# Delta's short convolution and its filters on TensorE, with part of the quantising and the first context groups sent ahead

## The chip, the cores and the metric

The kernel runs on one core of one Trainium2 chip, all of it in fp32 and in one launch. The metric is the time of one execution on the device, in microseconds (us); lower is better. A core has TensorE (PE), VectorE (DVE), ScalarE (ACT), GpSimd (POOL) and the sync engine (SP), each with its own stream of instructions, and 16 DMA engines that all queues share. The changed kernel runs under the same conditions.

## The reference, cut to what matters

The program is a Perceiver with four layers of three blocks each on `x` [128, 256] and a context `ctx` of 12544 rows of 256. Each block is `x = x + block(layernorm(x))`. The blocks that the change touches:

```
# layer 0: slot attention over ctx (3 iterations), parameter attention, then a quantised FFN
w  = clip(round(wb / s), -8, 7) * s     # blocks of 32 weights, s = max|wb| / 7, for w_up, w_gate, w_down
# layer 1: softmax attention over ctx with padding, then folded attention and experts
# layer 2: 16-head attention over ctx with a mask, then the delta block:
q = silu(dwconv(h @ Wq, conv_w_q))      # causal, depthwise, 4 taps; k and v likewise
beta = sigmoid(h @ Wb)
inv = solve_triangular(I + tril(kb @ k.T, -1), I)          # q, k normalised per head, kb = k * beta
delta_out = tril(q @ k.T) @ (inv @ (v * beta))             # 4 heads of 64; what crosses chunks is elided
local_short = dwconv(v, fir_short_w)    # 5 taps
local_long  = dwconv(v, fir_long_w)     # 64 taps
o = gated sum of local_short, local_long, delta_out, v;  o = rmsnorm(o) @ Wo
# layer 3: softmax attention over ctx (plain), multi-query attention, hashed experts
```

## The kernel before, in words

Twelve stages run one after the other: slots, patt (parameter attention), quant (the quantised FFN), padded, folded, moe, cross, delta, local, plain, mqa, hashed. A stage is one `nc.Block` in which each engine has its own program, written by hand in the order in which it runs; semaphores order the engines within a stage, and a barrier stands between stages. All stages but slots start with the layer norm of `x_kept` on DVE and ACT. Weights live in one region of SBUF (`K.weights`, `HOMES`; `weights_region` in rows) and are fetched by a DMA issued a stage or more ahead, mostly from SP's queue.

The context is read in 14 groups of 896 rows (`GROUPS`, `GROUP`). In padded and plain, `CtxAttention.sync` sends the transposed group `ctxT`, double buffered, from the start of its own stage; `CtxAttention.tensor` scores a group (`product`, L142), turns the probabilities (L1016) and attends (L1027). The cross stage projects keys and values of each group on PE into a ring of banks (L142, `cross_ring`), scores with 16 heads in sets (L1761) and DVE takes masked maxima in halves (L1921). There the SP queue holds `w_delta`, then `ctxT` and the mask of each group in turn, and POOL turns each mask into fp32 (L1725).

In patt, DVE quantises all weights of the FFN between its other work: `quantise_some(n)` takes the next n of 42 steps, 7 kinds (L757 to L769) on 6 pieces of 768 columns, and `Q_SPLIT` says how many go at each of nine places. In quant, PE transposes the quantised weights in lots of three (L913), ACT copies them out (L895), and the activations are quantised by a maximum over all partitions, which POOL makes (L904).

In delta, PE makes q, k and v with channels in the rows. DVE does the 4-tap convolution as 24 instructions (`tap`, L2188 for a first tap, L2189 for the others), ACT the sigmoid (L2146), PE transposes the product into token rows (L2074, L2076), and DVE normalises q and k (to L2230). The filters of 5 and 64 taps are 138 more instructions of `tap`, put by `filter_some` between the steps of the inverse. The inverse of `I + A` is built in 6 levels, each with the chain: DVE `E` (L2250), PE `E I` (L2098), DVE copy (L2253), PE `I E I` (L2108, L2109), DVE two subtractions (L2262, L2263). After it come `u` (L2113, L2266) and `delta_out` (L2117), then the statistics and gates of the four branches. `idle_products` (L158) are products whose result nobody reads.

## Time and profile before

| | |
|---|---|
| median of 3 runs | 1695.83 us (1695.51 to 1701.81) |
| profiled execution, its own time | 1700.65 us |
| its span | 1698.9 us |
| PE, DVE, ACT busy in the span | 1443.1, 966.7, 713.4 us |
| mean granted TensorE clock | 0.915 |

The profile is one execution, 4.8 us (0.3%) above the median; 1.8 us of its own time lie outside its span. Busy shares are means over twelve stages with different limits, so each stage is read by itself. The stages start, by their layer norms, at about 338 (patt), 405 (quant), 448 (padded), 562 (folded), 618 (moe), 689 (cross), 1304 (delta), 1434 (local), 1542 (plain), 1650 (mqa) and 1677 us (hashed).

### The profile page before, as it was taken

The numbers are of one execution on the slowest core, as the hardware profiler recorded it, in microseconds if no ns is written. First come the engines' busy times: TensorE is split into PE (matmuls) and PEld (weight loads), VectorE is DVE, ScalarE is ACT, GpSimd is POOL, SyncE is SP. The second block draws the span as 40 slices with busy tenths as digits, with TensorE's granted clock in tenths as the row PEclk, the third lists the DMA queues.
The fourth block names the chain that finished last, engine by engine and source line by source line (L and its number), as shares of the span: only waits on it lengthen the run. The fifth ranks groups of instructions, "written<-read, shape, count | busy, mean of one in ns | idle before, by whom it ended". The sixth has DMA issues, their size and how long they took to land. (4 is left out here: it accounts for less than half of the span.)

```text
span 1698.9 us, 28391 instructions
## 1 busy us (share of the span) xinstructions
PE 1443.1 (85%) x10880; PEld 1076.8 (63%) x10880; DVE 966.7 (57%) x2914; ACT 713.4 (42%) x1618; POOL 91.9 (5%) x86
## 2 busy tenths in 40 slices
PE   7999989886499867799999999999995455677997
PEld 6878979763267643467777777777764352545765
DVE  4654444465566312367777777777774873453433
ACT  5745535422122100166666666666663101212222
POOL 2300000000000200200000000000000000000000
PEclk9999999977699879899999999999998565998998
DMA  9935424110332469410010100000002002506830
GB/s 324 328 143 193 152 68 150 49 51 20 120 135 87 173 250 392 180 42 34 34 34 34 34 34 34 34 34 34 2 1 121 1 0 87 227 0 240 274 108 4
DMA packets 63318, 181.16 MB, mean 107 GB/s; under 512 B 7248, under 2 KB 43216, under 8 KB 61904
## 3 DMA queue, kind: packets, MB, share of 16 engines
q1 hardware_dynamic: 59488, 160.96, 26.4%
q0 software_dynamic: 3264, 12.58, 1.9%
q10 hardware_dynamic: 432, 5.80, 0.8%
q8 instruction: 88, 1.44, 0.3%
q14 instruction: 46, 0.38, 0.1%
HBM read 178.68 MB, written 0.66 MB: 106 GB/s over the span
## 5 line engine op out<-in xcount | busy, mean ns | idle before, releaser
L1849 ACT ACTIVATE cross_s<-cross_s,cross_shift 128x896 f32<-128x896 f32 x224 | 215.1, 1031 | 35.1 <-DVE cross_shift L1930 35.1
L1843 ACT COPY cross_eT<-cross_ring 128x512 f32<-128x512 f32 x280 | 153.1, 591 | 145.1 <-PE cross_ring L1769 145.1
L1769 PEld LDWEIGHTS cross_ring<-consts,cross_s 128*128 128x128 f32 x1568 | 170.8, 142 | 59.1 <-issue 43.8
L1769 PE MATMUL cross_ring<-consts,cross_s 128*128 128x128 f32 x1568 | 199.4, 280 | 8.7 <-ACT cross_s L1849 8.7
L1921 DVE CUSTOM_DVE_ANT_0 cross_s<-cross_scores,cross_mask,cross_top 128x448 f32<-128x448 f32 x224 | 141.3, 681 | 84.3 <-PE cross_scores L1761 84.3
L387 ACT ACTIVATE slots_probs<-slots_scores,slots_bias,ctx_rinv 128x128 f32<-128x128 f32 x294 | 130.1, 461 | 111.4 <-DVE slots_bias L432 111.4
L1921 DVE CUSTOM_DVE_ANT_0 cross_s<-cross_scores,cross_mask,cross_half_max 128x448 f32<-128x448 f32 x224 | 141.2, 680 | 18.9 <-PE cross_scores L1761 18.9
L142 PE MATMUL slots_scores<-slots_qkT,slots_ctxT 128*128 128x128 f32 x1176 | 140.9, 279 | 10.1 <-DMA slots_ctxT<-in_ctxT 9.3
L142 PEld LDWEIGHTS slots_scores<-slots_qkT,slots_ctxT 128*128 128x128 f32 x1176 | 139.4, 195 | 14.0 <-DMA slots_ctxT<-in_ctxT 10.2
L337 PE MATMUL slots_attended<-ctx_rows,slots_probs 128*128 128x257 f32 x588 | 135.1, 380 | 1.4 <-DVE slots_pooled L446 1.4
L1761 PE MATMUL cross_scores<-cross_keysT,cross_qz 32*128 32x448 f32 x896 | 119.1, 589 | 0.8 <-DVE cross_keysT L1895 0.8
L337 PEld LDWEIGHTS slots_attended<-ctx_rows,slots_probs 128*128 128x128 f32 x588 | 108.2, 190 | 17.7 <-DVE slots_probs L442 3.6
L428 DVE TENSOR_REDUCE slots_top<-slots_scores 128x7 f32<-128x896 f32 x42 | 45.9, 1092 | 116.8 <-PE slots_scores L142 116.7
L1783 PEld LDWEIGHTS cross_attended<-cross_eT,cross_values 128*32 128x32 f32 x3136 | 82.3, 110 | 37.9 <-issue 35.8
L1783 PE MATMUL cross_attended<-cross_eT,cross_values 128*32 128x128 f32 x3136 | 97.2, 274 | 2.3 <-ACT cross_eT L1843 1.7
L142 PE MATMUL cross_ring<-cross_ctxT,weights_region 128*128 128x448 f32 x224 | 92.0, 555 | 6.8 <-DMA cross_ctxT<-in_ctxT 6.8
L1903 DVE COPY cross_eT<-cross_ring 128x512 f32<-128x512 f32 x112 | 77.4, 691 | 35.5 <-PE cross_ring L1769 35.5
L142 PE MATMUL cross_ring<-weights_region,cross_ctxT 128*128 128x256 f32 x392 | 90.9, 384 | 0.0
L142 PEld LDWEIGHTS cross_ring<-weights_region,cross_ctxT 128*128 128x128 f32 x392 | 72.3, 190 | 10.4 <-issue 0.7
L1725 POOL TENSOR_SCALAR cross_mask<-cross_mask_int 128x896 f32<-128x896 int32 x14 | 44.9, 3207 | 471.0 <-DVE cross_top L1921 460.9
L142 PEld LDWEIGHTS cross_ring<-cross_ctxT,weights_region 128*128 128x128 f32 x224 | 41.3, 194 | 41.2 <-issue 32.9
L387 ACT ACTIVATION_READ_ACCUMULATOR slots_probs<-slots_scores,slots_bias,ctx_rinv 128x1 f32 x294 | 61.1, 208 | 0.0
(762 smaller groups left out, 2073.2 us busy)
## 6 DMA issues: line engine op xcount, KB each, us to landing
slots_ctxT<-in_ctxT SPq DMA_DIRECT2D x42, 896.0 KB, 4.6
ctx_rows<-in_ctx_rows SPq DMA_DIRECT2D x28, 896.0 KB, 7.1
padded_ctxT<-in_ctxT SPq DMA_DIRECT2D x14, 896.0 KB, 4.6
cross_ctxT<-in_ctxT SPq DMA_DIRECT2D x14, 896.0 KB, 4.6
plain_ctxT<-in_ctxT SPq DMA_DIRECT2D x14, 896.0 KB, 4.6
ring_w<-in_moe_w POOLq DMA_DIRECT2D x12, 1024.0 KB, 16.2
ring_w<-in_moe_w SPq DMA_DIRECT2D x12, 1024.0 KB, 10.9
local_layers<-in_w_local SPq DMA_DIRECT2D x2, 4806.0 KB, 14.1
```

The costliest lines, as they stand in the source:

```text
L142: last = pe.matmul(out, lhs, rhs, start=i == 0, stop=i == len(pairs) - 1)
L337: last = pe.matmul(at[b], probs[:, n % HELD, t], K.ctx[:, g * TILE + t, :], start=t == 0, stop=t == TILE - 1)
L387: last = act.activation(probs[:, a, t], sc[b][:, t], ACT.Exp, bias=bias[:, a, t:t + 1], scale=K.rinv[:, g * TILE + t:g * TILE + t + 1], ac ...
L428: dve.tensor_reduce(top[:, a], sc[b], X_AXIS, ALU.max).then_inc(st("top"), 1)
L1725: pool.tensor_scalar(mask[:, g % 2], mask_int[:, g % 2], 0.0, MASKED, ALU.is_equal, ALU.mult).then_inc(st("mask"), 1)
L1761: pe.matmul(scores(j), qz[rows, s // 2, s % 2], keysT[rows, g % 2, s // 2, half_keys(half)], start=True, stop=True).then_inc(st("scored"), 1)
L1769: last = pe.transpose(bank(("turn", u, t))[:, j * P:(j + 1) * P], s_buf[:, u % 2, j, t * P:(t + 1) * P], K.ident)
L1783: last = pe.matmul(attended[COLS * j:COLS * (j + 1), s * P:(s + 1) * P], values[:, g % 2, t, set_head(s, j)], eT[:, u % 2, t, j * P:(j + 1 ...
L1843: act.copy(eT[:, u % 2, t], bank(item)).then_inc(st("emptied_act"), 1)
L1849: act.activation(rows, rows, ACT.Exp, bias=shift[:, u % 2, j:j + 1], scale=SCALE).then_inc(st("exp"), 1)
L1903: dve.tensor_copy(eT[:, u % 2, t], bank(item)).then_inc(st("emptied_dve"), 1)
L1921: dve.tensor_tensor_reduce(s_buf[:, u % 2, j, half_keys(half)], scores(j), mask[:, g % 2, half_keys(half)], 1.0, so_far, ALU.add, ALU.max, ...
```

## The change

The change has four parts.

**Delta.** The 24 taps of the convolution and the 138 of the filters become 162 PE matmuls of 128x128 with a diagonal matrix that holds the tap's weights. ACT makes the diagonals (L2229 of the kernel after, `identity * scale`) into a ring of 40 places in the weights region; each tap waits for its diagonal, and diagonal n of 40 or more waits until tap n - 40 is done. q and k leave the convolution with tokens in the rows, so their four transposes, the copy and the product `qkvT` go. DVE only copies the two filtered branches from a bank at the end, after all 162 taps.

**Quantising.** `w_up` gets its own home and fetch, issued on ACT's queue behind `w_patt` at the start of the second slots iteration; DVE quantises it in the slots stage, one or two steps of 128x384 per group, 28 in all. In patt 28 steps of 768 columns are left, in the places 2, 4, 4, 2, 2, 3, 4, 5, 2, and the transposes of `up` move from quant into patt, in place of idle products.

**Early groups.** Two groups of `ctxT` for padded, one for cross, two for plain are fetched into the weights region in the stage before (quant, moe and local). padded and plain have 4 idle products at their start. In cross, the keys of group 0 are projected from there, four pieces of them (`BANKS` = 3 ahead of the layer norm's transposes, then one), DVE stores them before it makes `qz`, and `ctxT` of group 0 leaves SP's queue.

**The fetch of `w_hashed`** moves from the local stage to the end of plain's SP queue.

```diff
+def filter_taps():
+
+    return [(kind, c, k) for kind, rows, length in (("conv", 3 * DC, CONV), ("long", DC, LONG), ("short", DC, SHORT))
+            for c in range(rows) for k in range(length)]
+
+
+DIAGONALS = 40
 
 
...
+                fir_places = iter(enumerate(taps_in_turn))
+                for n, (_, ac, k) in itertools.islice(fir_places, 3 * DC * CONV):
+                    a, c = ac // DC, ac % DC
+                    pe.wait_ge(st("raw"), a + 1)
+                    pe.wait_ge(st("diagonal"), n + 1)
+                    shifted, diagonal = raw[:, a, c, k:k + P], diagonals[:, n % DIAGONALS]
+                    if a < 2:
+                        last = pe.matmul(b[4][:, ac * P:(ac + 1) * P], shifted, diagonal, start=k == 0, stop=k == CONV - 1)
+                    else:
+                        last = pe.matmul(b[5][:, c * P:(c + 1) * P], diagonal, shifted, start=k == 0, stop=k == CONV - 1)
+                    last.then_inc(st("filtered"), 1)
                 pe.wait_ge(st("silu"), 1)
...
+                def filter_some(count):
+
+                    for n, (kind, c, k) in itertools.islice(fir_places, count):
+                        pe.wait_ge(st("diagonal"), n + 1)
+                        length, at = (SHORT, c * P) if kind == "short" else (LONG, D + c * P)
+                        lo = PAD - length + 1 + k
+                        pe.matmul(b[7][:, at:at + P], vT[:, c, lo:lo + P], diagonals[:, n % DIAGONALS],
+                                  start=k == 0, stop=k == length - 1).then_inc(st("filtered"), 1)
+
+                filter_some(22)
                 pe.wait_ge(st("unit"), 1)
                 for c in range(DC):
                     for a, src in ((0, qk[:, 0]), (1, qk[:, 1])):
...
-                    if n == LEVELS - 1:
-                        pe.wait_ge(st("firs"), 1)
-                        for a in range(2):
-                            for c in range(DC):
-                                last = pe.transpose(b[1][:, (a * DC + c) * P:(a * DC + c + 1) * P], firs[:, a, c], K.ident)
-                        last.then_inc(st("firs_mm"), 1)
+                    filter_some(4)
                     pe.wait_ge(st("EI"), n)
...
+                    filter_some(8)
...
+                filter_some(len(taps_in_turn))
                 pe.wait_ge(st("u"), 1)
...
+                def diagonal_some(count):
+
+                    for n, (kind, c, k) in itertools.islice(diagonal_places, count):
+                        if n >= DIAGONALS:
+                            act.wait_ge(st("filtered"), n - DIAGONALS + 1)
+                        act.activation(diagonals[:, n % DIAGONALS], K.ident, ACT.Copy, scale=taps_of[kind][:, c, k:k + 1]).then_inc(st("diagonal"), 1)
+
+                diagonal_some(DIAGONALS)
+                act.wait_ge(st("filtered"), 2 * DC * CONV)
+                act.activation(act_sig[:, 0:2].rearrange("p a d -> p (a d)"), b[4][:, :], ACT.Sigmoid).then_inc(st("sigmoid"), 1)
+                act.wait_ge(st("filtered"), 3 * DC * CONV)
+                act.activation(act_sig[:, 2], b[5][:, 0:D], ACT.Sigmoid).then_inc(st("sigmoid"), 1)
                 act.wait_ge(st("beta_mm"), 1)
...
+                act.wait_ge(st("sumsq"), 1)
+                act.activation(norms[:, 1, :], norms[:, 0, :], ACT.Sqrt).then_inc(st("lengths"), 1)
+                diagonal_some(len(taps_in_turn))
...
-                    filter_some(8)
                     dve.wait_ge(st("EI_mm"), n)
                     dve.tensor_copy(EI[:, :], two(b[4][:, :])).then_inc(st("EI"), 1)
-                    filter_some(14)
...
+                dve.wait_ge(st("filtered"), len(taps_in_turn))
+                link(dve.tensor_copy(z[:, 0:2].rearrange("p a h d -> p (a h d)"), b[7][:, :]))
...
-Q_SPLIT = (4, 8, 4, 2, 2, 4, 4, 4, 10)
+Q_SPLIT = (2, 4, 4, 2, 2, 3, 4, 5, 2)
...
+                        if it == 1 and 3 <= g < GROUPS:
+                            up.some(dve, 1)
+                        if it == 2 and g < GROUPS:
+                            up.some(dve, 2 if g < 4 else 1)
...
-                idle_products(pe, K, spare, 2)
+                turn_up(0)
+                turn_up(1)
...
-                idle_products(pe, K, spare, 4)
+                turn_up(2)
+                turn_up(3)
+                idle_products(pe, K, p_idle, 2)
...
+                K.weights.wait(pe, "cross")
+                for p in range(BANKS):
+                    project(("keys", 0, p))
                 pe.wait_ge(st("ln_done"), 1)
...
-                K.weights.fetch(sp, "hashed")
+                K.weights.fetch_early(sp, "plain")
...
+EARLY = {"padded": 2, "cross": 1, "plain": 2}
```

On PE, in one level of the inverse of the kernel before (`delta_bank` is the bank that a matmul writes; the pair L2108, L2109 comes once for each head, four times in all), the rows are:

```order
L2098 MATMUL delta_bank<-delta_inv,delta_E 128x128 x4
L2108 MATMUL delta_bank<-delta_EI,delta_inv 128x128
L2109 MATMUL delta_bank<-delta_inv,delta_EI 128x128
...
L2098 MATMUL delta_bank<-delta_inv,delta_E 128x128 x4
```

On the same engine the kernel after has, from the end of qkv to the first level, these rows; `weights_region` here is the ring of diagonals, `delta_raw` and `delta_vT` what is filtered:

```order
L155 MATMUL delta_bank<-weights_region,delta_hT 128x4 x2
L2137 MATMUL delta_bank<-weights_region,delta_raw 128x128 x16
L2139 MATMUL delta_bank<-delta_raw,weights_region 128x128 x8
L2143 MATMUL delta_bank<-consts,delta_vT 128x128 x2
L2152 MATMUL delta_bank<-weights_region,delta_vT 128x128 x22
L2159 MATMUL delta_bank<-consts,delta_qk 128x128 x2
...
L2152 MATMUL delta_bank<-weights_region,delta_vT 128x128 x6
...
L2152 MATMUL delta_bank<-weights_region,delta_vT 128x128 x24
L2178 MATMUL delta_bank<-delta_inv,delta_E 128x128 x4
L2152 MATMUL delta_bank<-weights_region,delta_vT 128x128 x4
L2183 MATMUL delta_bank<-delta_EI,delta_inv 128x128
L2184 MATMUL delta_bank<-delta_inv,delta_EI 128x128
...
L2152 MATMUL delta_bank<-weights_region,delta_vT 128x128 x8
L2178 MATMUL delta_bank<-delta_inv,delta_E 128x128 x4
```

So taps of L2152 stand now ahead of products that the chain waits for: 22 before the transposes of q and k (L2159), 6 and 24 about the products of A (L2170), then 4 and 8 in every level.

On ACT, from the start of delta, the kernel before has:

```order
L180 ACTIVATE delta_ln_mv<-delta_ln_mv 128x1
L2146 ACT_TABLE_LOAD
L2146 ACTIVATE delta_act_sig<-delta_act_in 128x768
L2148 ACTIVATE delta_beta<-delta_bank 128x4
L2149 ACTIVATE delta_res<-weights_region 128x4
L2151 ACTIVATE delta_temp<-weights_region 128x1
L2152 ACT_TABLE_LOAD
L2152 ACTIVATE delta_temp<-delta_temp 128x1
L2153 ACT_TABLE_LOAD
L2153 ACTIVATE delta_temp<-delta_temp 128x1
L2155 ACT_TABLE_LOAD
L2155 ACTIVATE delta_norms<-delta_norms 128x8
```

and the kernel after has there:

```order
L193 ACTIVATE delta_ln_mv<-delta_ln_mv 128x1
L2229 ACTIVATE weights_region<-consts,weights_region 128x128 x40
L2233 ACT_TABLE_LOAD
L2233 ACTIVATE delta_act_sig<-delta_bank 128x512
L2235 ACTIVATE delta_act_sig<-delta_bank 128x256
L2237 ACTIVATE delta_beta<-delta_bank 128x4
L2238 ACTIVATE delta_res<-weights_region 128x4
L2241 ACT_TABLE_LOAD
L2241 ACTIVATE delta_norms<-delta_norms 128x8
L2229 ACTIVATE weights_region<-consts,weights_region 128x128 x122
L2243 ACTIVATE delta_temp<-weights_region 128x1
L2244 ACT_TABLE_LOAD
L2244 ACTIVATE delta_temp<-delta_temp 128x1
L2245 ACT_TABLE_LOAD
L2245 ACTIVATE delta_temp<-delta_temp 128x1
```

So 40 diagonals stand ahead of the first table load and the sigmoids, and 122 behind the lengths of q and k.

## Rows read from the trace of the kernel before

**Rows 1.** Windows: length, busy of PE, PEld, DVE, ACT, POOL, clock, DMA, GB/s

```profile
689.00:1304.00 615.00, 589.70 (x6348) 419.07 (x6348) 430.80 (x1625) 401.46 (x580) 48.40 (x18) 0.98 0.10 37
1304.00:1434.00 130.00, 65.67 (x268) 51.72 (x268) 90.41 (x265) 12.89 (x21) 0.26 (x2) 0.57 0.10 40
```

**Rows 2.** Timeline of delta, head: start, us, engine, line, [idle before <-releaser]

```profile
1311.20 1.34 DVE L2183 COPY delta_raw<-delta_bank 128x256 f32<-128x256 f32 x3 [4.53 <-PE delta_bank L142]
...
1313.76 4.81 DVE L2189 SCALAR_TENSOR_TENSOR delta_act_in<-delta_raw,weights_region,delta_act_in 128x128 f32<-128x128 f32 x18
...
1319.94 0.84 ACT L2146 ACTIVATE delta_act_sig<-delta_act_in 128x768 f32<-128x768 f32 x1
...
1328.33 0.42 DVE L2230 TENSOR_TENSOR delta_kb<-delta_qk,delta_beta 128x256 f32<-128x256 f32 x1
```

**Rows 3.** Timeline of delta, the levels and what follows them

```profile
1341.18 0.69 DVE L2250 TENSOR_TENSOR delta_E<-delta_A,weights_region 128x512 f32<-128x512 f32 x1
...
1350.80 2.08 PE L2098 MATMUL delta_bank<-delta_inv,delta_E 128*128 128x128 f32 x8 [2.23 <-DVE delta_E L2250]
...
1353.65 0.80 PE L2108 MATMUL delta_bank<-delta_EI,delta_inv 128*128 128x128 f32 x2 [0.78 <-DVE delta_EI L2253]
...
1359.67 1.16 PE L2098 MATMUL delta_bank<-delta_inv,delta_E 128*128 128x128 f32 x8 [2.23 <-DVE delta_E L2250]
...
1393.79 1.10 PE L2113 MATMUL delta_bank<-delta_vb,delta_inv 128*128 128x64 f32 x8 [1.57 <-DVE delta_inv L2263]
...
1395.48 1.97 PE L2117 MATMUL delta_bank<-delta_u,delta_attnT 128*128 128x64 f32 x8 [0.59 <-DVE delta_u L2266]
```

**Rows 4.** Timeline of patt: ACT on 128x128 tiles with a scalar from memory

```profile
357.49 4.23 ACT L526 ACTIVATE patt_pr<-patt_scores,patt_small 128x128 f32<-128x128 f32 x16 [5.58 <-DVE patt_small L536]
```

**Rows 5.** Windows of two stretches, columns as in rows 1

```profile
1342.00:1350.00 8.00, 5.78 (x24) 5.19 (x24) 7.69 (x25) 0.00 (x0) 0.00 (x0) 0.50 0.00 0
...
490.00:510.00 20.00, 20.00 (x86) 14.25 (x85) 13.73 (x30) 5.12 (x12) 0.00 (x0) 1.00 0.41 138
```

**Rows 6.** Timeline of cross, start

```profile
701.07 8.54 PE L142 MATMUL cross_ring<-cross_ctxT,weights_region 128*128 128x448 f32 x16 [6.84 <-DMA cross_ctxT<-in_ctxT]
702.91 6.53 POOL L1725 TENSOR_SCALAR cross_mask<-cross_mask_int 128x896 f32<-128x896 int32 x2 [10.03 <-DMA cross_mask_int<-in_mask]
...
718.68 0.68 DVE L1921 CUSTOM_DVE_ANT_0 cross_s<-cross_scores,cross_mask,cross_half_max 128x448 f32<-128x448 f32 x1 [4.69 <-PE cross_scores L1761]
```

**Rows 7.** DMA view: transfers, count, KB each, us from issue to landing

```profile
weights_region<-in_w_hashed SPq DMA_DIRECT2D x1, 5764.0 KB, 33.1
...
weights_region<-in_w_delta SPq DMA_DIRECT2D x1, 2596.5 KB, 10.0
```

**Rows 8.** Timeline of patt: quantising steps and a product

```profile
359.94 3.52 DVE L757 TENSOR_REDUCE block_max<-weights_region 128x24 f32<-128x768 f32 x4
...
397.62 1.90 PE L738 MATMUL patt_scores<-weights_region,patt_efT 128*128 128x256 f32 x8
398.70 5.29 DVE L769 TENSOR_TENSOR weights_region<-weights_region,block_max 128x768 f32<-128x768 f32 x6
```

**Rows 9.** Timeline of padded, start

```profile
453.15 4.90 PE L142 MATMUL padded_scores<-padded_ctxT,padded_hT 128*128 128x512 f32 x8 [2.58 <-DMA padded_ctxT<-in_ctxT]
...
468.87 0.98 PE L1016 MATMUL padded_turned<-consts,padded_e 128*128 128x128 f32 x7 [1.24 <-ACT padded_e L1047]
```

**Rows 10.** Timeline of plain, start

```profile
1546.23 9.40 PE L142 MATMUL plain_scores<-plain_ctxT,plain_hT 128*128 128x512 f32 x16 [2.18 <-DMA plain_ctxT<-in_ctxT]
```

**Rows 11.** Timeline of slots and quant

```profile
136.86 3.39 PE L142 MATMUL slots_scores<-slots_qkT,slots_ctxT 128*128 128x128 f32 x28 [1.68 <-DMA slots_ctxT<-in_ctxT]
...
165.03 1.09 DVE L428 TENSOR_REDUCE slots_top<-slots_scores 128x7 f32<-128x896 f32 x1 [3.10 <-PE slots_scores L142]
...
412.89 0.38 POOL L904 PARTITION_ALL_REDUCE quant_small<-quant_small  x1 [315.48 <-issue]
```

**Rows 12.** The page's costliest groups: the line's weight loads

```profile
L1769 PEld LDWEIGHTS cross_ring<-consts,cross_s 128*128 128x128 f32 x1568 | 170.8, 142 | 59.1 <-issue 43.8
```

More of the change, by code:

```diff
@@ L645, in stage_pattention @@
         spare = mm[:, 1024:1536]
+        up_n = K.weights.buf("quant_up").rearrange("p (o i) -> p o i", i=D)
+        upT = K.weights.beyond("quant", DC * QFFN).rearrange("p (c o) -> p c o", c=DC)
+        p_idle = mm[:, 1536:2048]
+        lots = [(c, o, (spare, sc[:, 1024:1536])[n % 2]) for n, (c, o) in enumerate((c, o) for c in range(DC) for o in (0, 3))]
         with nc.Block() as block:
@@ L688, in mask, with turn_up @@
                     pe.matmul(heads[:, 4 * g:4 * g + 4], K.ident, repeat(K.causal, 4), start=True, stop=False)
+                def turn_up(n):
+                    c, o, bank = lots[n]
+                    if n >= 2:
+                        pe.wait_ge(st("up_copied"), n - 1)
+                    for j in range(3):
+                        last = pe.transpose(bank[:, j * P:(j + 1) * P], up_n[:, o + j, c * P:(c + 1) * P], K.ident)
+                    last.then_inc(st("up_mm"), 1)
                 turn("k", "k_probs")
@@ L1006, in score @@
             for lo, hi in ((0, KEYS_A), (KEYS_A, GROUP)):
-                last = product(pe, self.sc[b][:, lo:hi], [(self.qT[:, c], ctxT[:, b, c, lo:hi]) for c in range(DC)])
+                last = product(pe, self.sc[b][:, lo:hi], [(self.qT[:, c], ctxT[:, c, lo:hi]) for c in range(DC)])
             last.then_inc(st("scored"), 1)
@@ L1794, in spread_decay @@
                     last.then_inc(st("filled"), 1)
-                for p in range(KEY_PIECES):
-                    project(("keys", 0, p))
                 pe.wait_ge(st("qz"), 1)
@@ L1943, in add @@
                     dve.wait_ge(st("added"), g + 1)
-                for p in range(KEY_PIECES):
-                    store(("keys", 0, p))
                 for u in range(STEPS + 2):
@@ L2781 @@
 }
+EARLY = {"padded": 2, "cross": 1, "plain": 2}
+EARLY_AT = {"padded": HOMES["padded"][1] + width(PADDED_SPEC), "cross": HOMES["cross"][1] + width(CROSS_SPEC) + SLOT_W1 + SLOT_W2,
+            "plain": HOMES["hashed"][1]}
 REGION = max(at + width(spec) for spec, at in HOMES.values())
```

292 lines of the change are left out of this document (145 added, 147 removed).

## The prediction

> **What bounds the kernel now.** I read the page first, then the windows by stage, then the timeline of each stage that the change touches, and last the DMA view. The stages stand one behind the other, so each has its own bound and the gains add. In cross PE is busy 589.70 of 615 us: only its start can give. In delta PE is busy 65.67 of 130 us at a granted clock of 0.57, and DVE 90.41 [rows 1]. The timeline of delta shows two reasons. At its head PE waits for DVE's 24 taps, which end at 1318.6 [rows 2]. In the levels it is a chain: E, product, copy, product, two subtractions. DVE's filter taps fill only the waits of that chain, so removing them alone gains almost nothing; but PE runs its two products at the low level of its clock: eight records in 2.08 us, against 1.16 us in a level that had the high one [rows 3]. So what counts in delta is the clock, and the chain at its head. Padded and plain lose time at their start to groups of the context that are still on their way.
>
> **Delta, the head.** A product is two records: (1.16 - 0.3 for the end of the last one) / 4 gives 0.21 us a tap at the high level (2.4 GHz), (2.08 - 0.37) / 4 gives 0.43 at the low one (1.2 GHz) [rows 3]. A diagonal costs ACT 4.23 / 16 = 0.264 us, by 16 instructions of the same size that also take a scalar from memory [rows 4]. From about 1305.1, behind the layer norm, 40 of them end at 1315.7. The first copies of `raw` are done at 1311.6 [rows 2], so the 16 taps of q and k are through at 1315.0 and the 24 at 1316.7: ACT is later than PE. The sigmoid stood 1.3 us behind the last tap, a table load, so it starts at 1317.0 and, for 512 of 768 columns at 0.84 us [rows 2], ends at 1317.6, against 1320.8. From there to the end of `kb` it was 8.0 us (to 1328.75) [rows 2]; without the transposes of q and k, the wait for them and their copy it is 5.9: 1323.5, a gain of 5.2. But 22 taps stand ahead of the transposes that wait for it. They start at about 1321.2 and take 4.7 us, to 1325.9, and give back 2.4. Then the transposes and the products of A run at the high level, which gives about 1.7; the 6 taps lie beside DVE's copies, the 24 (5.1 us) beside DVE's ten instructions for A (5.7 us). The first E starts at 1336.7 instead of 1341.18 [rows 3]: **-4.5**.
>
> **Delta, the levels.** Six levels took from 1341.18 to 1393.79, 52.6 us, 8.8 each [rows 3]. At the high level the products give back 0.92 and twice that: 8.9 - 2.7 = 6.2 us. The 4 taps, 0.85 us, stand where PE waited 0.78 for DVE's copy, the 8, 1.7 us, where it waited 2.23 [rows 3]: I put 6.3 a level, 37.8 in all: **-14.8**. Is the clock high? PE would be busy over 90% of such a level. The stretches show 1.00 where PE is busy without a gap, and 0.50 where it is busy 5.78 of 8 us [rows 5]; at low clock the taps would leave PE no gap at all, which is the first case. I take the high level. Behind `u`'s product stand the last 162 - 148 = 14 taps, 3.0 us, ahead of `delta_out`'s product, which waited 0.6 for `u`, and itself becomes shorter by about 1 [rows 3]: +1.3. For 162 waits on a diagonal I add 1. **Delta: -17**. Its bounds: -21 if the waits cost nothing and all of A runs at the high level; -8 if two levels fall to the low one, at 11.0 us each (below).
>
> The Trainium skill ("ScalarE: Activation LUTs", What ACT_TABLE_LOAD costs) has about 280 ns plus 0.833 ns a column for an ACTIVATE with one pointer operand, less 93 ns back to back, or 0.294 us a diagonal where the row shows 0.264: by it 40 diagonals end 1.2 us later, and the sum would be 1 less.
>
> **Cross.** Projecting the keys of group 0 began at 701.07, when its group landed, at low clock (8.54 us) [rows 6]; it can now begin at about 688.5, right behind moe and before the layer norm. The mask comes next: in SP's queue it stands directly behind `w_delta`, issued at 688.9, which takes 10.0 us [rows 7]; the mask then took 702.91 - 701.07 = 1.8, so it lands at 700.7, POOL turns it in half of 6.53 [rows 6], and DVE's first maxima start at 704.0, four of 0.68 us later the second half at 706.6. That half started at 718.68 [rows 6], after PE had done the values; these now lie before the mask. From there the chain is the same and PE stays full to the end of the stage: -12.1, and **-11.5** for DVE's stores that now stand in its way. Bounds: -9.5 (mask and early group meet on the DMA engines, 2 us), -12.7 (all of 701.07 - 688.4).
>
> **Patt.** A quantising step of 768 columns costs DVE 3.52 / 4 = 0.88 us [rows 8]. Two steps fewer stand before the copies of the probabilities: -1.75; one fewer before the sum with `xin`: -0.9. At the end, f's product was done at 399.5 and DVE with six steps at 404.0 [rows 8]; two steps are left, and five instead of four before the last copy delay the product by 0.6: -3.9. The moved transposes take PE 6 records where four of twice the width stood: nothing. **-6.5**, from -4.5 (a stretch more at low clock) to -8.
>
> **Padded and plain.** In padded the turn of group 1 waited to 468.87, 1.24 us of it for ACT [rows 9]. Scores waited 2.58 for their first group [rows 9] and again for the second. With both there, they start some 2.0 us earlier and run on, and DVE's and ACT's chain on group 1 begins some 5.8 earlier, which sets that turn: **-5.5** (-3.7 if the products run low, -6.3). In plain the scores waited 2.18, and the sixteen records took 9.40, half of it at low clock [rows 10]; 1.6 of the wait go, and the idle products keep the clock up for about 3: **-4.5** (-2.5 to -5.5).
>
> **The rest.** In slots the 28 steps on half the columns, 0.45 us each, lie in 3.10 us that DVE waits in each group [rows 11]; but 768 KB more are fetched, and PE already waited 1.68 for a group behind `w_patt` [rows 11]: +0.5 (0 to +1.5). In quant POOL's first all-reduce starts at 412.89, about when the lots ended [rows 11]; it sets the products, so fewer lots gain nothing, and less work for PE may cost clock: +0.5 (0 to +1.5). `w_hashed`, 33.1 us with company [rows 7], is sent at about 1620 and needed at 1677 less the gains: nothing, with over 10 us of cover.
>
> **Sum.** 0.5 - 6.5 + 0.5 - 5.5 - 11.5 - 17 - 4.5 = -44. The profiled execution would go from 1700.65 (span 1698.9) to 1656.7 (span 1655). The median lies 4.8 below that execution: 1695.83 - 44 = **1652**.
>
> **Rivals.** (1) *The clock stays low in delta.* For: 0.57 over the stage. Against: the work without a gap. 22 taps are then 9.4 us and hold the transposes, 24 are 10.2 and hold the first product of a level: it starts 9.8 later than before. A level takes 8.9 + (1.7 - 0.8) + (3.4 - 2.2) = 11.0, six of them 13 more than before; 14 taps add 5.4. Delta +28 in place of -17: 1697, no change. Chance 0.05.
>
> (2) *Each tap runs alone*, because it waits for a semaphore and bumps one. A record alone is a weight load of 142 ns [rows 12] and a product of some 0.28, so a tap 0.84. On the path are 164 t - 31 us of taps (148 filter taps less 25.4 of cover, 16 of q and k less 5.4), against -22.6 with no taps at all: at t = 0.84, +84 in delta, 1753, slower. It decides from t = 0.49, where delta's +27 eats the rest. Against: the waits are on work long done, as the ring runs 40 ahead. Chance 0.04.
>
> (3) *The early groups give little*: transfers collide, idle products stand before the layer norm's transposes (8 records of 256 columns took 1.90 in patt [rows 8], and twice that at the low level), cross wins 5, padded and plain 1 each: 1666. Chance 0.13.
>
> (4) *The best ends of all bounds*, a sum of -55: 1641. Chance 0.06.
>
> **How the numbers follow.** The forecast has 0.72. The range goes from rival 4 to the sum of the poor ends (-22, or 1674), and so takes in rival 3: 1640 to 1673. 0.5% is 8.5 us, about what a measurement here can tell. Faster: forecast, rivals 3 and 4, 0.91; no change 0.05; slower 0.04.
>
> **What would show it.** PE's clock in delta near 1 from about 1310 to 1375; first E near 1337, levels of 6.3 us; taps 0.21 us apart; cross's second half of maxima near 12 us earlier against its stage; DVE's last steps of patt end with f's product. A tap spacing over 0.3, or a clock of 0.6 in the levels, would make the prediction wrong.

## The result, and the profile after

The changed kernel takes 1654.88 us (median of 4 runs, 1649.57 to 1658.64), the kernel before 1695.67 beside it; the ratio is 0.9756, 95% interval 0.9712 to 0.98. Predicted were 1652 us and a range of 1640 to 1673. A later measurement of the same two kernels, 5 runs against 9, gave 0.9767 (0.9746 to 0.9789).

The profiled execution has a span of 1647.8 us, 51.1 below that of before, where the medians are 40.8 apart: the one of before lies 5.0 us above this median, the one of after is the fastest of its four, 5.3 below its own. A second profile of the same kernel (experiment 12) has a span of 1650.8. So the stages are read from both, from one layer norm's start to the next. The last column is the span; folded, mqa and hashed, which are left out, are together 3.7 and 2.2 us shorter than before:

| kernel | slots | patt | quant | padded | moe | cross | delta | local | plain | span |
|---|---|---|---|---|---|---|---|---|---|---|
| before | 334.1 | 66.8 | 43.2 | 113.9 | 70.7 | 615.0 | 130.2 | 107.5 | 108.3 | 1698.9 |
| after | 331.0 | 57.2 | 47.9 | 107.7 | 69.2 | 605.0 | 111.6 | 108.6 | 103.8 | 1647.8 |
| after, second profile | 334.3 | 55.6 | 46.8 | 107.7 | 70.1 | 605.9 | 110.2 | 109.3 | 103.8 | 1650.8 |

A stage that is not changed also varies from profile to profile. Over the profiles of the kernel after and of its edits in other stages, patt took 54.7 to 57.3 us, quant 45.9 to 48.4, cross 605.0 to 608.8, delta 108.5 to 111.6 and local 107.7 to 114.6; padded took 107.7 every time, plain 103.7 or 103.8 and once 105.2. In a second profile with the stages of before (experiment 1, where only delta is edited) patt took 64.3, quant 43.2 and cross 615.3. Experiments 1 to 10 are one execution each, and only their stages are compared.

The windows of the kernel after, for patt, quant, cross and delta, in the columns of [rows 1]:

```profile
335.00:392.00 57.00, 46.67 (x180) 32.46 (x180) 36.49 (x80) 16.13 (x41) 0.00 (x0) 0.80 0.08 28
392.00:440.00 48.00, 20.42 (x60) 12.11 (x60) 21.56 (x43) 7.66 (x15) 1.78 (x5) 0.64 0.15 56
...
672.00:1277.00 605.00, 588.57 (x6348) 417.10 (x6348) 430.63 (x1625) 401.55 (x580) 48.41 (x18) 0.99 0.10 36
1277.00:1389.00 112.00, 83.45 (x584) 71.61 (x584) 48.15 (x102) 62.00 (x185) 0.26 (x2) 0.83 0.12 46
```

In delta PE has 17.8 us more work than in [rows 1] and the stage is 18.6 us shorter: the granted clock went from 0.57 to 0.83. DVE lost 42 us of work. The six levels by themselves, in the kernel before and the kernel after:

```profile
1341.18:1393.79 52.61, 33.77 (x148) 30.53 (x148) 46.11 (x136) 0.00 (x0) 0.00 (x0) 0.58 0.00 0
```

```profile
1309.45:1346.93 37.48, 34.52 (x288) 33.08 (x289) 16.55 (x24) 25.38 (x77) 0.00 (x0) 1.00 0.01 1
```

The timeline of delta, kernel after, weight loads left out:

```profile
1277.97 11.78 ACT L2229 ACTIVATE weights_region<-consts,weights_region 128x128 f32<-128x128 f32 x40
...
1291.06 0.60 ACT L2233 ACTIVATE delta_act_sig<-delta_bank 128x512 f32<-128x512 f32 x1
...
1294.83 5.08 PE L2152 MATMUL delta_bank<-weights_region,delta_vT 128*128 128x128 f32 x44
...
1296.91 0.42 DVE L2292 TENSOR_TENSOR delta_kb<-delta_qk,delta_beta 128x256 f32<-128x256 f32 x1
1299.74 0.38 PE L2159 MATMUL delta_bank<-consts,delta_qk 128*128 128x128 f32 x2
...
1309.45 0.69 DVE L2310 TENSOR_TENSOR delta_E<-delta_A,weights_region 128x512 f32<-128x512 f32 x1
1310.20 1.16 PE L2178 MATMUL delta_bank<-delta_inv,delta_E 128*128 128x128 f32 x8 [0.89 <-DVE delta_E L2310]
1311.20 1.06 PE L2152 MATMUL delta_bank<-weights_region,delta_vT 128*128 128x128 f32 x8
...
1314.04 1.95 PE L2152 MATMUL delta_bank<-weights_region,delta_vT 128*128 128x128 f32 x16
...
1315.68 0.69 DVE L2310 TENSOR_TENSOR delta_E<-delta_A,weights_region 128x512 f32<-128x512 f32 x1
1316.42 1.16 PE L2178 MATMUL delta_bank<-delta_inv,delta_E 128*128 128x128 f32 x8 [0.44 <-DVE delta_E L2310]
...
1347.77 3.34 PE L2152 MATMUL delta_bank<-weights_region,delta_vT 128*128 128x128 f32 x28
...
1350.95 1.00 PE L2194 MATMUL delta_bank<-delta_u,delta_attnT 128*128 128x64 f32 x8
```

Against [rows 3] the first product of a level takes 1.16 us every time, and a level 6.22 (1309.45 to 1315.68) where it was 8.8. The 22 taps ahead of the transposes (44 records) hold PE for 4.9 us, from 1294.83 to 1299.74: 0.22 us each, wait for the diagonal included. `kb` ends at 1297.33, but the transposes that wait for it start at 1299.74, because the taps stand in front of them. At the end u is copied at 1348.5, and `delta_out`'s product waits to 1350.95, behind 14 taps.

Cross, kernel after: the early keys, POOL's first mask, the second half of DVE's maxima:

```profile
672.11 4.75 PE L155 MATMUL cross_ring<-weights_region 128*128 128x448 f32 x12 [1.19 <-PEq L1476]
...
686.53 6.53 POOL L1786 TENSOR_SCALAR cross_mask<-cross_mask_int 128x896 f32<-128x896 int32 x2 [10.63 <-issue]
...
692.41 0.68 DVE L1991 CUSTOM_DVE_ANT_0 cross_s<-cross_scores,cross_mask,cross_half_max 128x448 f32<-128x448 f32 x1
```

The keys run at the stage's start, but POOL's conversion of the mask starts 14.6 us behind it, no earlier than before (13.9, [rows 6] against 689.0). Quant, kernel after:

```profile
402.83 0.38 POOL L953 PARTITION_ALL_REDUCE quant_small<-quant_small  x1 [309.70 <-issue]
...
406.03 5.49 PE L155 MATMUL quant_mm_gate<-quant_gateT,quant_hT 128*128 128x512 f32 x8 [0.59 <-DVE quant_hT L995]
```

POOL's first all-reduce (the maximum over all partitions) comes 10.6 us behind the stage's start, where [rows 11] have 8.0 (412.89, from 404.9). The end of patt and the starts of padded and plain:

```profile
389.16 2.00 PE L814 MATMUL patt_scores<-weights_region,patt_efT 128*128 128x256 f32 x8 [0.45 <-DVE patt_efT L896]
391.20 0.48 DVE L899 SCALAR_TENSOR_TENSOR x_kept<-patt_scores,patt_root,x_kept 128x256 f32<-128x256 f32 x1 [0.36 <-PE patt_scores L814]
...
440.17 1.96 PE L171 MATMUL padded_turned<-consts 128*128 128x256 f32 x8 [0.99 <-PEq L933]
...
1497.27 3.42 PE L171 MATMUL plain_turned<-consts 128*128 128x256 f32 x8 [1.91 <-PEq L2437]
...
1501.70 6.28 PE L155 MATMUL plain_scores<-weights_region,plain_hT 128*128 128x512 f32 x16 [0.59 <-DVE plain_hT L1276]
```

DVE now waits for f's product, where before the finished product waited for DVE; and plain's sixteen records of scores take 6.28 where [rows 10] have 9.40, though the idle products themselves ran at the low clock there (3.42 us; padded's same eight took 1.96).

### The profile page after: what moved, and what is told of

Its sections match the earlier page's. It is cut to its first block and busy times, and to the rows that moved or that the text cites. A ratio compares the mean times of both kernels' runs of the same rounds, so it can differ in the third digit from the quotient of the medians.

```text
span 1647.8 us, 29080 instructions
## 1 busy us (share of the span) xinstructions
PE 1446.8 (88%) x11204; PEld 1088.0 (66%) x11204; DVE 926.8 (56%) x2764; ACT 762.1 (46%) x1782; POOL 91.8 (6%) x86
## 5 line engine op out<-in xcount | busy, mean ns | idle before, releaser
L386 PEld LDWEIGHTS slots_attended<-ctx_rows,slots_probs 128*128 128x128 f32 x588 | 108.3, 190 | 17.5 <-DVE slots_probs L494 3.4
L480 DVE TENSOR_REDUCE slots_top<-slots_scores 128x7 f32<-128x896 f32 x42 | 45.9, 1092 | 101.7 <-PE slots_scores L155 101.7
L155 PE MATMUL cross_ring<-cross_ctxT,weights_region 128*128 128x448 f32 x208 | 85.7, 556 | 0.0
L155 PE MATMUL cross_ring<-weights_region,cross_ctxT 128*128 128x256 f32 x364 | 84.6, 384 | 0.0
L155 PEld LDWEIGHTS cross_ring<-weights_region,cross_ctxT 128*128 128x128 f32 x364 | 67.0, 190 | 9.1
L1830 PEld LDWEIGHTS cross_scores<-cross_keysT,cross_qz 32*128 32x128 f32 x896 | 37.9, 183 | 42.3 <-issue 30.5
```

Source lines behind the costliest of these rows:

```text
L155: last = pe.matmul(out, lhs, rhs, start=i == 0, stop=i == len(pairs) - 1)
L386: last = pe.matmul(at[b], probs[:, n % HELD, t], K.ctx[:, g * TILE + t, :], start=t == 0, stop=t == TILE - 1)
L480: dve.tensor_reduce(top[:, a], sc[b], X_AXIS, ALU.max).then_inc(st("top"), 1)
L1830: pe.matmul(scores(j), qz[rows, s // 2, s % 2], keysT[rows, g % 2, s // 2, half_keys(half)], start=True, stop=True).then_inc(st("scored"), 1)
```

## The experiments

**1. The kernel before without its filter taps.** Is it DVE's load or PE's clock that sets the levels?

```diff
-    for k in range(LONG // 2):
-        for c in range(DC):
-            yield LONG_FIR, c, k
-            yield LATE_FIR, c, LONG // 2 + k
...
+    for c in range(DC):
+        yield LONG_FIR, c, 0
+        yield LATE_FIR, c, LONG // 2
+    for c in range(DC):
+        yield SHORT_FIR, c, 0
```

> The kernel before with 132 of the 138 filter taps on DVE left out (the output is not the reference's there); the first tap of each of six chains stays. Theory A (the levels are a chain, DVE's taps only fill its waits, and PE's clock sets the length): DVE's work in the levels falls by more than half, PE's does not change, so a level stays at 8.2 to 8.9 us and the delta stage at 125 to 130 us (it was 130.2). Rival B (the taps in DVE's queue delay its copies and subtractions): a level falls below 7.5 us and the stage by 8 us or more.

Measured: delta 129.2 us, levels of 8.5 on average. The window of delta, and PE's first product of a level:

```profile
1299.00:1429.00 130.00, 66.65 (x268) 51.27 (x268) 56.47 (x135) 12.90 (x21) 0.26 (x2) 0.57 0.10 40
```

```profile
1354.46 2.08 PE L2096 MATMUL delta_bank<-delta_inv,delta_E 128*128 128x128 f32 x8 [2.22 <-DVE delta_E L2245]
```

DVE is busy 56 us in place of 90, and the stage is 1.0 us shorter. The 132 taps cost DVE 34 us and the stage 1: theory A.

**2. The kernel after without its filter taps on PE.**

```diff
-    return [(kind, c, k) for kind, rows, length in (("conv", 3 * DC, CONV), ("long", DC, LONG), ("short", DC, SHORT))
+    return [(kind, c, k) for kind, rows, length in (("conv", 3 * DC, CONV), ("long", DC, 1), ("short", DC, 1))
...
```

> The kernel after with the two filters cut to one tap each (4 taps in place of 138; the output is not the reference's there). The convolution stays on PE. Theory A (it is the taps' own work on PE that keeps the granted clock at the high level, which is what shortens the levels): without them PE falls to the low level in the levels for most of the time, and a level takes 7.5 to 8.8 us in place of 6.22; the stage, in spite of 134 products less, is 3 to 12 us longer than 111.6. Rival C (the clock stays high by itself once it is high, or the levels are short for another reason): a level stays at 6.1 to 6.3 us, and the stage falls by 4 to 5 us, since no tap stands in the way at the head and at the end.

Measured: delta 123.0 us, 11.4 longer than with 134 taps more (the unchanged stage takes 108.5 to 111.6), and levels of 8.5 on average. Its window and one level:

```profile
1287.00:1411.00 124.00, 72.08 (x316) 57.89 (x316) 48.16 (x103) 22.49 (x51) 0.26 (x2) 0.60 0.10 42
```

```profile
1336.38 0.69 DVE L2310 TENSOR_TENSOR delta_E<-delta_A,weights_region 128x512 f32<-128x512 f32 x1
...
1344.63 0.69 DVE L2310 TENSOR_TENSOR delta_E<-delta_A,weights_region 128x512 f32<-128x512 f32 x1
```

The clock is 0.60 against 0.83. So the taps on PE are worth more as work that keeps the clock up than as work taken from DVE: theory A again, at the upper end of its size. Set beside experiment 1, where the filters are gone too but the convolution is still on DVE (129.2), this also splits the gain: the convolution on PE is worth some 6 us and the filter taps on PE some 11, by one profile each.

**3. Quant's transfers behind the first all-reduce.**

```diff
+                sp.wait_ge(st("all_max"), 1)
                 K.weights.fetch(sp, "padded")
                 K.weights.fetch_early(sp, "padded")
```

> The kernel after, with all three transfers of the quant stage sent only after the first maximum over all partitions. Theory D (POOL's first all-reduce was late, 10.6 us behind the start of the stage against 8.0 before, because what POOL has to load for it shares the DMA engines with the early groups): it starts 5.5 to 8.0 us behind the start of the stage, and the stage falls from 47.9 to 43 to 45.5 us. Rival E (POOL takes its time whatever the DMA engines do): it starts 10 to 11 us behind the start, and the stage stays at 47 to 49 us. In both, padded stays within 1 us of 107.7.

Measured: quant 42.3 us, padded 107.7 as in the kernel after. The all-reduce of this kernel starts 6.5 us behind the stage's start (393.8):

```profile
400.24 0.38 POOL L954 PARTITION_ALL_REDUCE quant_small<-quant_small  x1 [305.76 <-issue]
```

Theory D holds for all three transfers together: sent at the stage's start, they cost 4.1 us by this POOL instruction. The early groups have the larger part of that, 2.6, since with the first transfer alone, as in the kernel before, it came at 8.0. Of the remaining 1.5 us, 0.9 lie in the gate's products, which take 4.59 us here and 5.49 in the kernel after, with more of them at the low clock.

**4. The delta weights behind two groups in cross's queue.**

```diff
-                K.weights.fetch(sp, "delta")
                 for g in range(GROUPS):
+                    if g == 2:
+                        K.weights.fetch(sp, "delta")
```

> The kernel after, with the fetch of the delta weights moved behind the first two groups of context and mask in SP's queue of the cross stage. Theory F (the first mask was late because it shares the DMA engines with 2.6 MB of weights and a third group, so that it lands when all of them are through, 14.6 us behind the stage's start): POOL's first conversion starts 4 to 7 us behind the start, DVE's first maxima 9.5 to 11 us behind it in place of 18.0, and the stage falls from 605.0 to 597 to 600 us. Rival G (POOL itself was late, not the mask): the conversion still starts 14 to 15 us behind the start and the stage stays at 604 to 606 us.

Measured: cross 606.7, and POOL's first conversion 16.1 us behind the start (678.03). The row, and the window before it:

```profile
694.16 6.53 POOL L1787 TENSOR_SCALAR cross_mask<-cross_mask_int 128x896 f32<-128x896 int32 x2 [12.21 <-issue]
```

```profile
692.00:694.00 2.00, 2.00 (x11) 1.77 (x10) 0.00 (x0) 0.75 (x2) 0.00 (x0) 1.00 0.24 94
```

Theory F fell: the order in the queue does not matter, and the mask is not what is waited for. It landed 3.1 us after its issue, and POOL took it up 13 us later; in the kernel after it took 9.6 us to land, and POOL started 4.6 us behind that. In the nine profiles whose cross stage is as in the kernel after, the conversion starts 14.6 to 16.6 us behind the start, so 16.1 is no change. POOL started when the DMA engines had run empty (their share falls to 0.24 in that window, after about 1 in the ten microseconds before).

**5. The delta weights and the third group only behind the first mask.** As 4, with `sp.wait_ge(st("mask"), 1)` ahead of the moved fetch.

> The kernel after, with the delta weights and the third context group of the cross stage sent only after POOL has made the first mask, so that just 1.8 MB (a group and two masks) are under way at the start. Moving the weights to the end of the first batch had left POOL's first conversion at 15.8 us behind the stage's start. Theory H (POOL starts that instruction only once the DMA engines have run empty, whatever stands in their queues): 1.8 MB take some 5 us, so the conversion starts 6 to 9 us behind the start, DVE's first maxima 10 to 13 in place of 18.0, and the stage falls from 605.0 to 597 to 601 us. Rival G (POOL is late by itself): it stays at 14 to 16 us behind the start, and the stage at 604 to 607 us.

Measured: cross 601.2 (-3.8, and below all nine of the unchanged stage), the first conversion 11.7 us behind the start (675.75). The transfers are through by 682, and POOL starts at 687.4:

```profile
682.00:684.00 2.00, 1.26 (x9) 0.88 (x8) 1.25 (x4) 0.00 (x0) 0.00 (x0) 1.00 0.00 0
```

```profile
687.44 6.53 POOL L1788 TENSOR_SCALAR cross_mask<-cross_mask_int 128x896 f32<-128x896 int32 x2 [7.75 <-issue]
```

Between H and G: less traffic brings it forward by 3 us, not by 6 to 8. The last 5.4 us, with idle DMA engines, stay open, and so does the reason why traffic delays POOL at all. It is not that POOL starts late as a whole: its memsets began 0.4 us behind the stage's start.

**6. Fewer taps ahead of the transposes.**

```diff
-                filter_some(22)
+                filter_some(12)
...
-                filter_some(24)
+                filter_some(27)
...
-                    filter_some(8)
+                    filter_some(9)
```

> The kernel after, with 12 in place of 22 filter taps ahead of the transposes of q and k in delta, 27 in place of 24 behind the products of A, and 9 in place of 8 behind I E I in each level; 15 instead of 14 are left for the end. Theory I (the 22 taps hold up those transposes by 2.4 us, and a level has 0.44 us in which PE waits for E, room for one more tap of 0.24 us): the transposes start 2.2 to 2.5 us earlier against the stage's start, a level stays at 6.2 to 6.3 us, and the stage falls from 111.6 by 1.5 to 2.5 us. Rival J (the taps only fill time, and each one moved comes back elsewhere; or the clock drops where PE now waits): levels of 6.45 us or more, and the stage within 0.7 us of 111.6 or longer.

Measured: the transposes start 20.5 us behind the stage's start in place of 22.75, levels stay at 6.22, and the statistics of `z` start 1.8 us earlier (73.7 us behind the start against 75.5); yet the stage is 111.6, as without the edit. Right behind the taps the transposes now run:

```profile
1302.98 2.84 PE L2152 MATMUL delta_bank<-weights_region,delta_vT 128*128 128x128 f32 x24
...
1305.66 0.38 PE L2159 MATMUL delta_bank<-consts,delta_qk 128*128 128x128 f32 x2
```

Theory I was right up to the levels' end. The gain went behind the statistics, 0.9 us in the gate's products and 0.9 in the logits' products after them: the clock stayed low there to the stage's end and beyond, 41.0 us on end, where the kernel after has it low in two stretches of 17.1 and 20.5 us with 3.4 high between. How much this can do shows in the profile of experiment 3, where delta is not edited and took 108.5 us: the gate's products took 7.4 us there in place of 10.6, because the clock was high in part of them.

**7. No idle products at the start of padded and plain.** The two lines `idle_products(pe, K, flash.turned, 4)` are taken out.

> The kernel after, without the 4 idle products at the start of padded and of plain. Theory K (they keep TensorE's clock at the high level for the first two lots of scores, worth more than the 1.5 us by which they hold up the transposes in plain): 16 records of scores take 8 to 12 us in place of 6.28, padded goes from 107.7 to 109 to 112 us and plain from 103.8 to 104.5 to 107. Rival L (the early groups alone bring the gain; the idle products cost): padded stays at 107.7 and plain falls to 102 to 103.

Measured: padded 110.6 (+2.9), plain 104.5 (+0.7). Plain's scores without them:

```profile
1508.44 8.37 PE L155 MATMUL plain_scores<-weights_region,plain_hT 128*128 128x512 f32 x16 [0.59 <-DVE plain_hT L1274]
```

Theory K: of padded's 6.2 us almost half is the clock. In plain, 2.1 us of clock are set against 1.5 us of delay; its +0.7 rests on one profile, and the unchanged stage has once taken 105.2.

**8. A first all-reduce that nobody reads.** Experiment 3, and `pool.partition_all_reduce(warm[:, 0:1], K.ident[:, 0:1], ...)` as POOL's first instruction of quant.

> The kernel with the transfers of quant behind the first all-reduce (42.3 us for the stage, first all-reduce 6.4 us behind its start), and with one more all-reduce on POOL, of a column that nobody reads, as POOL's first instruction of the stage. Theory M (the first all-reduce after a long pause costs POOL some 4 us of loading, and any one of the kind pays for it): the first one of use starts 3.0 to 5.0 us behind the stage's start, and the quant stage falls to 39.5 to 41.5 us. Rival N (the time belongs to each first use of new data, or is a wait for the maxima): it stays at 6 to 7 us and the stage at 42 to 43.

Measured: quant 42.4. The extra one starts no earlier than the real one did, 6.3 us behind the stage's start (396.8), and the real one at its heels:

```profile
403.07 0.38 POOL L953 PARTITION_ALL_REDUCE quant_warm<-consts  x1 [304.57 <-issue]
403.37 0.42 POOL L956 PARTITION_ALL_REDUCE quant_small<-quant_small  x1
```

The numbers are those of theory N, but each theory is half right. The second all-reduce follows the first by 0.3 us, so the time does not belong to each use of new data: the first of the kind pays. But it runs no earlier although it waits for no input, 6.3 us behind the start against 6.5 with its input ready at 2.2, so one more of the kind in the same stage cannot pay earlier.

**9. A shorter head.** 24 diagonals in place of 40 ahead of the sigmoid, its table loaded early, and 4 idle products at delta's start.

```diff
+                idle_products(pe, K, b[7], 4)
                 pe.wait_ge(st("ln_done"), 1)
...
-                diagonal_some(DIAGONALS)
+                diagonal_some(3 * DC * CONV)
+                act.activation(K.unused, K.ident[:, 0:1], ACT.Sigmoid)
...
+                diagonal_some(4)
```

> The kernel after, with three edits at the head of delta: 24 diagonals in place of 40 stand ahead of the first sigmoid, the sigmoid table is loaded by a one-column sigmoid before the wait for the taps, and 4 idle products at the start hold TensorE's clock for the q, k and v products. Theory O (the 40 diagonals, 11.8 us of ACT at 0.294 each, set the sigmoid, not PE's taps): the first sigmoid of 512 columns ends 11 to 12.5 us behind the stage's start in place of 14.7, the transposes of q and k start 20.0 to 21.5 in place of 22.75 behind it, and the stage falls from 111.6 by 1.5 to 3 us, if the clock in the rest of the stage stays as it was. Rival P (PE's products and taps set it, and ACT only looks late): the sigmoid ends at 14 or later, and the stage stays within 0.7 us.

Measured: delta 112.7; the sigmoid ends 14.9 us behind the start. That is P's number for the sigmoid (the stage is 1.1 us longer, outside P's 0.7), but the run does not test O cleanly: the idle products found the clock low, took 3.75 us and held up the layer norm's transposes by 1.8 us.

```profile
1283.45 3.75 PE L171 MATMUL delta_bank<-consts 128*128 128x256 f32 x8 [0.99 <-PEq L1764]
...
1301.49 2.85 PE L2153 MATMUL delta_bank<-weights_region,delta_vT 128*128 128x128 f32 x23
```

The taps of q and k were through 1.5 us later and the sigmoid only 0.2. In the kernel after, the 40 diagonals and these taps both end 12.8 us behind the start: ACT and PE bound the head equally, and 24 diagonals with the table loaded early could give no more than the table load, 1.3 us (an estimate from these rows; no run has that edit alone). The filter taps, with no stock of diagonals, ran at ACT's pace from the twelfth on, 0.29 us a tap.

**10. Half the gate products ahead of the statistics.**

```diff
+                gate_banks = (b[4], b[6])
+                for c in range(DC):
+                    for k in range(DC):
+                        pe.matmul(gate_banks[c][:, :].rearrange("p (h k) -> p h k", k=P), w1[:, k, c * P:(c + 1) * P],
+                                  hT[:, k].unsqueeze(1).to_broadcast([P, HEADS4, P]), start=k == 0, stop=False)
                 pe.wait_ge(st("stats"), 1)
...
+                    last = pe.matmul(gate_banks[c][:, :].rearrange("p (h k) -> p h k", k=P), W["w1s"][0:GATE_IN, cols], statsT[:, :],
+                                     start=False, stop=True)
```

> The kernel after, with the half of delta's gate product that needs only the layer norm's output (4 products of 512 columns, 7.6 us at the low clock) issued behind delta_out's product, into two banks that are free there, while DVE makes the statistics. Theory Q (behind the levels PE rests for 8 us, its clock falls, and 10.8 us of gate products then run at the low level on the path): the products behind the statistics take 1.2 to 3.3 us in place of 11 to 12, and the stage falls from 111.6 to 102 to 105.5 us. Rival R (the freed time is lost elsewhere: ACT, the clock of what follows): the stage falls by less than 4 us.

Measured: delta 107.3 (-4.3). The moved half runs at the high clock; the four products that need the statistics still at the low one, since PE rests 4.5 us for them:

```profile
1360.03 3.65 PE L2200 MATMUL delta_bank<-delta_hT,weights_region 128*128 128x512 f32 x8
...
1369.96 3.78 PE L2209 MATMUL delta_bank<-delta_statsT,weights_region 16*128 16x512 f32 x4 [0.77 <-DVE delta_statsT L2349]
```

Q in kind, R's limit nearly in size: the 3.78 was put at 1.2 to 3.3, and 0.9 went in the logits' products behind it. Against the kernel after, 5.9 us are gone from the start of the statistics' transposes on; the stage gained 4.3, because they started 1.6 us later here, at the end of a head and levels that are not edited.

**11. Four edits together**: 3, 5, 6 and 10, and 8 idle products ahead of the wait for the statistics.

> The kernel after with four edits together: quant's transfers behind the first all-reduce (-5.7 us in its stage when alone), the delta weights and the third group behind the first mask in cross (-3.8), 12, 27 and 9 filter taps in place of 22, 24 and 8 in delta, and the first half of the gate products ahead of the statistics, with 8 idle products behind them that keep TensorE's clock high until the statistics are there (-4.3 for the gate alone, without idle products). If the gains add: quant 42 to 43 us, cross 600 to 602, delta 102 to 106, and 14 to 19 us less than the kernel after in all, so some 1637 us beside 1654, and a ratio to the kernel before of 0.964 to 0.969. If the clock takes them back (as it took the 1.8 us of the taps when these were moved alone): delta 107 or more and 9 to 11 us less than the kernel after in all.

**12. The kernel after once more**, beside it.

> The kernel after once more, beside the kernel with the four edits on the same chip, so that the two can be compared, and to see how far its stages scatter from one run to the next. Expected: 1650 to 1659 us, a ratio of 0.973 to 0.979 to the kernel before, quant 46 to 48.5 us, delta 110 to 112, plain 103.8, and 2 to 6 us of scatter in slots, moe and local, which this change does not touch or hardly.

Measured: 1637.53 us (1635.57 to 1640.76, 5 runs) against 1656.23 (1652.60 to 1662.30, 5 runs) and 1696.43 for the kernel before (9 runs). The ratios to the kernel before are 0.9655 (0.9638 to 0.9672) and 0.9767 (0.9746 to 0.9789): 18.7 us less than the kernel after. Quant 42.3, cross 601.3, delta 104.4. In delta, the idle products (16 records) and what follows the statistics:

```profile
1350.71 3.62 PE L171 MATMUL delta_bank<-consts 128*128 128x256 f32 x16
...
1356.75 1.98 PE L2213 MATMUL delta_bank<-delta_statsT,weights_region 16*128 16x512 f32 x4 [0.77 <-DVE delta_statsT L2353]
```

The four products that took 3.78 us in experiment 10 take 1.98: here the clock was still high. Delta is 7.2 us shorter than in the kernel after, and 4.1 below the shortest of the unchanged stage. From the statistics' transposes on 8.1 us are gone, against 5.9 in experiment 10, and the 2.2 more came with the idle products. What the moved taps gave does not show: the statistics started 0.9 us later than in the kernel after.

## Why the prediction was right, step by step

- **Delta, -17 predicted, -18.6 and -20.0 measured.** The first E was to come 4.5 us earlier against the stage's start: 4.8 and 3.1. Levels of 6.3 us: 6.22. The clock's part was tested from both sides (experiments 1 and 2). Three terms were mis-sized and nearly cancelled. A diagonal costs 11.78 / 40 = 0.294 us, not 0.264 as 16 instructions of [rows 4] have it, and q's, k's and v's products took 5.46 us, partly at the low clock, so the sigmoid ended 14.7 us behind the start instead of 13.7. From the transposes to the first E it was 9.7 us instead of 10.8. And 1 us was added for the taps' waits, which cost nothing beside the 0.22 us of a tap. By the figures of the Trainium skill ("ScalarE: Activation LUTs", What ACT_TABLE_LOAD costs) the estimate for such an instruction, back to back, is 0.294 us, and this trace agrees. The 2.4 us given back by the 22 taps, and 1.3 at the tail (measured 1.6), came as worked out.
- **Cross, -11.5 predicted, -9.9 and -9.1 measured.** The step that failed: "the mask lands at 700.7, POOL turns it, and DVE's first maxima start at 704.0". They started 18.0 us behind the stage's start instead of 15.0, and the second half 20.5 instead of 17.6. The mask did land early enough, 9.6 us after its issue; but POOL's instruction was taken to start when its mask is there, and it came when all transfers had landed. As many bytes are under way there as before, since the third group is now sent at once too. That traffic is a cause is shown (experiments 4 and 5), how it acts is not.
- **Patt, -6.5 predicted, -9.6 and -11.1 measured.** The three places gave what DVE's steps were worth (-1.8, then the sum with `xin` at 39.9 us behind the stage's start against 44.5, and -5.0 from there to its end). The low clock holds 22.6 us of the stage in place of 32.7, and the eight records of f's first products, for one, take 5.29 us in place of 6.38. But part of the excess is the profile of before: the other one has this stage at 64.3 us with 26.7 at the low clock, and against it the gain is 7.1 and 8.7. That less waiting for DVE keeps PE's clock up, which the sum leaves out, fits these numbers; no run isolates it.
- **Quant, +0.5 predicted (0 to +1.5), +4.8 and +3.6 measured: outside its bounds.** The step "it sets the products, so fewer lots gain nothing" was right, but the all-reduce was taken as fixed. It depends on the DMA traffic: 6.3 to 6.5 us behind the stage's start with none, 8.0 with the 0.8 MB of before, 10.4 to 11.1 with the early groups. The gate's products, 5.49 us in place of 4.38 at a lower clock, are half of the rest.
- **Padded, -5.5 predicted, -6.2 measured; plain, -4.5 predicted, -4.5 measured.** As worked out; experiment 7 splits them: the idle products are 2.9 of the one and 0.7 net of the other.
- **Slots, +0.5 predicted; -3.1 and +0.3 measured.** The longer wait for a group is there (3.0 us in place of 1.7, in the second iteration), but this stage scatters by more, 331 to 338 us over all runs. Moe, where the change only adds a transfer, varies from 68.9 to 73.2, and local from 107.5 to 114.6.
- **The sum**, -44, was close to the medians' -40.8 and, later, -40.2. In the two pairs of profiles quant's +4 and cross's +2 stand against patt's -4 and delta's -2, so it was right in its mechanisms and large terms, and lucky in the small ones. Those pairs add up to -51.1 and -48.1, more than the medians show, since the profile of before lies above its median and those of after lie below theirs; which stage holds the 3 us by which the medians fell short can't be told from them. Rivals 1 and 2 are excluded by the clock of 1.00 in the levels and taps of 0.22 us; rival 3 holds for a part of cross only. The ends of the range were added wrongly: its best bounds sum to -53.5, not -55, and its poor ones to -25.2, not -22. That gives 1642 to 1671, and the measured time lies inside that too.

## What to carry to other kernels

Where a chain of small products alternates with another engine, look at the granted clock of that stretch first: work that is moved onto PE into the chain's gaps can pay twice, once for the engine that it leaves (1 us here, for the filters) and once for the clock (11.4 us), and work that is taken off PE can lengthen the chain. A transfer that is sent "ahead" into an idle moment can hold up whatever is small and urgent in it, here POOL's first all-reduce or conversion of a stage; send it behind that. When a gain of some us ahead of a stretch disappears, compare the clock behind it before looking for a new wait. And before a difference in one stage of one profile is believed, look how far that stage varies in profiles that leave it alone: 3.1 us here in delta.

## What the runs showed of the hardware that was not expected

- In quant, POOL's first all-reduce came 6.3 to 6.5 us behind the stage's start with no transfers sent, 8.0 with 0.8 MB (7.7 in experiment 1) and 10.4 to 11.1 with 2.6 MB, although what it waited for was ready at 2.2. Why is open.
- In cross, the order of transfers in a queue did not decide when POOL, their reader, started (16.1 us with the mask first, 14.6 to 16.6 with the weights first); it started earlier with fewer bytes under way (11.7 with 1.8 MB).
- An ACTIVATE of 128x128 that reads its scale from memory took 0.294 us at the pace of 40 and more in a row.
- Idle products cost nearly twice their time if the clock is low when they start (3.75 and 3.42 us against 1.96 for the same 8 records): they are cheap where they keep the clock up, and dear where they find it low.
